# Linear attention and a routed feed-forward on one core: the routing stages run one slot nearer to the attention

## What is computed

```
x = x + attention(layernorm(x))      # 16 heads of 8, causal, scores without softmax: (Q K^T * causal) V, then w_o
x = x + experts(layernorm(x))        # logits = layernorm(x) @ Wg, softmax over 8 experts, the best 2 of each token
                                     # y = p * (relu(xs @ W1[e] + b1[e]) @ W2[e] + b2[e]), both choices added up
```

## Time and profile before

| | |
|---|---|
| median of 3 runs | 280.29 us (279.5 to 280.4) |
| the profiled execution | 280.46 us |
| its span, first to last instruction | 278.7 us |
| TensorE, busy share | 82% |
| VectorE | 73% |
| ScalarE | 61% |
| GpSimd | 65% |
| mean granted clock of TensorE | 0.916 |

### The profile page before, as it was taken

How to read it: one execution, slowest core, us unless ns; L and a number is a source line. 1 busy time by engine, 2 the same in 40 slices (tenths; PEclk the granted TensorE clock), 3 DMA queues, 4 the chain that set the end, 5 groups by cost and what they waited for, 6 DMA issues and landing times.

```text
span 278.7 us, 6426 instructions
## 1 busy us (share of the span) xinstructions
PE 227.6 (82%) x1418; PEld 175.7 (63%) x1418; DVE 202.1 (73%) x598; ACT 170.7 (61%) x675; POOL 182.0 (65%) x175
## 2 busy tenths in 40 slices
PE   6699889999999999998856279988919999999100
PEld 6354546666666666665545169877909999999000
DVE  5879999889989898999984848844502555554852
ACT  3543358888989898878697146655604767766000
POOL 3329961123868878687737777777777777777750
PEclk9999999999999999999995559999965999999855
DMA  6980000000100101011101272233445333438984
GB/s 203 280 246 0 2 1 0 2 0 12 41 30 30 41 30 42 29 38 39 51 29 48 67 166 69 59 105 103 115 131 142 107 98 88 125 101 294 330 228 136
DMA packets 32425, 25.49 MB, mean 91 GB/s; under 512 B 4334, under 2 KB 30192, under 8 KB 32390
## 3 DMA queue, kind: packets, MB, share of 16 engines
q1 hardware_dynamic: 23824, 14.52, 19.4%
q0 software_dynamic: 4320, 8.47, 9.1%
q10 hardware_dynamic: 4246, 2.10, 2.6%
HBM read 13.92 MB, written 11.61 MB: 92 GB/s over the span
## 4 chain that ended last, share of the span: by engine, by line
PE 55%; DVE 17%; DMA 10%; issue 8%; POOL 3%; ACT 3%; SPq 2%; POOLq 1%; DVEq 1%; ACTq 0%
PE ps L971 16%; PE ps L1063 8%; PE ps L1074 7%; PE ps L939 6%; DMA returned<-y_sb,xt 4%; POOL returned L417 3%; DVE back L680 3%; PE ps L980 2%; DMA xt<-dispatched 2%; PE ps L1056 2%; PE ps L991 2%; PE ps L962 2%; DVE back L671 2%; DVE o_sb L693 2%; PE ps L983 1%
## 5 line engine op out<-in xcount | busy, mean ns | idle before, releaser
L389 POOL DMA_INDIRECT dispatched<-rows,slot x64 | 65.8, 1028 | 37.5 <-ACT rows L482 17.0
L417 POOL DMA_INDIRECT returned<-y_sb,xt x71 | 71.1, 1002 | 21.6 <-issue 17.1
L971 PE MATMUL ps<-back,causal 128*128 128x512 f32 x128 | 61.9, 606 | 0.0
L881 DVE TENSOR_SCALAR y_sb<-ps,xt 128x128 f32<-128x128 f32 x71 | 24.9, 350 | 47.1 <-PE ps L1075 46.8
L1063 PE MATMUL ps<-xT,w_of 128*128 128x128 f32 x284 | 49.9, 301 | 1.2 <-DVE w_of L876 0.7
L1074 PE MATMUL ps<-w_sb,hT 128*128 x284 | 45.7, 285 | 0.1
L564 ACT ACTIVATE hT<-ps,b_col 128x128 f32<-128x128 f32 x142 | 44.2, 367 | 1.2 <-PE ps L1063 0.7
L373 POOL TENSOR_TENSOR back<-qkv 128x1024 f32<-128x1024 f32 x16 | 31.3, 1954 | 20.8 <-ACT qkv L503 20.6
L556 ACT ACTIVATE xT<-ps 128x128 f32<-128x128 f32 x71 | 19.7, 278 | 38.2 <-PE ps L1056 37.0
L1063 PEld LDWEIGHTS ps<-xT,w_of 128*128 128x128 f32 x284 | 39.8, 203 | 3.3 <-ACT xT L556 2.0
L680 DVE TENSOR_TENSOR back<-ps,qkv 128x1024 f32<-128x1024 f32 x32 | 38.9, 1216 | 2.1 <-PE ps L971 2.0
(11 more groups left out here) (171 smaller groups left out, 422.2 us busy)
## 6 DMA issues: line engine op xcount, KB each, us to landing
xt<-dispatched SPq DMA_DIRECT2D x71, 65.0 KB, 1.9
back<-returned SPq DMA_DIRECT2D x7, 512.0 KB, 6.4
x_sb<-x SPq DMA_DIRECT2D x8, 256.0 KB, 5.3
out<-x_sb ACTq DMA_DIRECT2D x7, 256.0 KB, 3.6
returned<-y_sb,xt POOLq DMA_INDIRECT x71, 2.5
w_sb<-w SPq DMA_DIRECT2D x1, 1024.0 KB, 5.7
w_sb<-w SPq DMA_DIRECT2D x2, 512.0 KB, 7.6
dispatched<-rows,slot POOLq DMA_INDIRECT x64, 2.3
```

The lines of the kernel that those rows point to most:

```text
L389: pool.indirect_dma_start(out=dispatched[:, :], out_offset=bass.IndirectOffsetOnAxis(ap=slot[:, g * K + k:g * K + k + 1], axis=0), in_=row ...
L417: pool.indirect_dma_start(out=returned[:, :], out_offset=bass.IndirectOffsetOnAxis(ap=xt[:, n % G, D:D + 1].bitcast(I32), axis=0), in_=y_s ...
L971: mm = pe.matmul(ps_run[g % 2][:, u, :], causal[:, :], outer[:, g % OUTER_RING, 512 * u:512 * (u + 1)], start=True, stop=True)
```

## The change

Every routing stage and every stage of the second normalization runs one slot earlier, on all engines: lags 10 to 13 of ScalarE become 9 to 12, 8 and 9 of VectorE become 7 and 8 (add_residual stays at 5), 10 to 12 of TensorE become 9 to 11, and dispatch(s - 16) becomes dispatch(s - 15). STATE_AFTER and the waits that name a tile go along. With that, softmax_end and places of batch 5 fall into VectorE's loop. In the tail VectorE makes the second statistics of the last six tiles, in two groups (26 and 27, then 28 to 31), and ScalarE's row_of is gone; softmax_start of batch 6 stands ahead of the last two tiles' residuals.

```
-    STATE_AFTER = 7
+    STATE_AFTER = 6
...
+    LAST = [range(N - 6, N - T), range(N - T, N)]
...
-            for s in range(N + 16):
-                if s >= 16:
-                    dispatch(s - 16)
+            for s in range(N + 15):
+                if s >= 15:
+                    dispatch(s - 15)
...
-            tile_stages = [(10, mean2_out), (12, exponentials), (10, spread2_out), (0, qkv_out), (10, variance_log2), (11, xn2T_out), (10, scale2_out),
-                           (-1, xnT_out), (10, shift2_out), (6, qT_out), (10, rows_out), (-2, normalize), (7, oT_out), (13, chosen),
+            tile_stages = [(9, mean2_out), (11, exponentials), (9, spread2_out), (0, qkv_out), (9, variance_log2), (10, xn2T_out), (9, scale2_out),
+                           (-1, xnT_out), (9, shift2_out), (6, qT_out), (9, rows_out), (-2, normalize), (7, oT_out), (12, chosen),
...
-            exponentials(N - 2 * T - 1)
-            xn2T_out(N - 8)
+            xn2T_out(N - 7)
             qT_out(N - 3)
+            chosen(N - 2 * T - 1)
             oT_out(N - 4)
             qT_out(N - 2)
-            row_of(N - 7)
             qT_out(N - 1)
             oT_out(N - 3)
-            chosen(N - 2 * T - 1)
-            row_of(N - 6)
+            last_deviation(0)
+            rows_out(N - 6)
             oT_out(N - 2)
-            row_of(N - 5)
+            rows_out(N - 5)
+            xn2T_out(N - 6)
             oT_out(N - 1)
-            xn2T_out(N - 7)
-            xn2T_out(N - 6)
             xn2T_out(N - 5)
-            last_deviation()
             exponentials(N - T - 1)
+            last_deviation(1)
...
-            tile_stages = [(5, add_residual), (9, softmax_end), (1, attend_sum), (8, softmax_start), (0, attend), (0, scales_ahead),
-                           (9, places), (2, state_out), (-2, outer_product), (-2, statistics_ahead)]
+            tile_stages = [(5, add_residual), (8, softmax_end), (1, attend_sum), (7, softmax_start), (0, attend), (0, scales_ahead),
+                           (8, places), (2, state_out), (-2, outer_product), (-2, statistics_ahead)]
...
             count_first()
+            add_residual(N - 5)
+            last_statistics(N - 6)
+            last_statistics(N - 5)
             state_out(N - 2)
-            add_residual(N - 5)
-            softmax_end(N - 2 * T - 1)
+            last_shift(0)
             attend_sum(N - 1)
             state_out(N - 1)
-            places(N - 2 * T - 1)
-            for g in range(N - T, N):
+            for g in range(N - 4, N - 2):
                 add_residual(g)
                 last_statistics(g)
-            last_shift()
             softmax_start(N - T - 1)
+            for g in range(N - 2, N):
+                add_residual(g)
+                last_statistics(g)
+            last_shift(1)
             softmax_end(N - T - 1)
...
-                wait(pe, shift_done, batches(g - 12))
+                wait(pe, shift_done, batches(g - 11))
...
-            tile_stages = [(3, running_sums), (11, gate), (5, q_transposed), (7, o_transposed), (5, sum_state), (-1, project),
-                           (-2, transpose1), (10, transpose2), (7, project_out), (12, rank)]
+            tile_stages = [(3, running_sums), (10, gate), (5, q_transposed), (7, o_transposed), (5, sum_state), (-1, project),
+                           (-2, transpose1), (9, transpose2), (7, project_out), (11, rank)]
```

More of the change, by code:

```diff
@@ L511, in exponentials, with last_deviation @@
                 act.activation(expd[:, :, :], shifted[:, :, :], ACT.Exp).then_inc(exp_done, 1)
[L513 to L517, removed]
+            def last_deviation(n):
+                own = LAST[n]
+                act.wait_ge(last_stats, own.stop - LAST[0].start)
+                act.activation(log2[:, own.start:own.stop], mv[:, own.start:own.stop, 1], ACT.Ln, bias=eps[:, 0:1]).then_inc(last_log, 1)
+                act.wait_ge(last_log, n + 1)
+                act.activation(norm2[:, own.start:own.stop, 0], log2[:, own.start:own.stop], ACT.Exp, scale=-0.5).then_inc(last_rstd, 1)
             def rows_out(g):
-                if g < N - T:
+                if g < LAST[0].start:
                     wait(act, norm2_done, g + 1)
                 else:
-                    act.wait_ge(last_norm, 1)
+                    act.wait_ge(last_norm, 1 + (g in LAST[1]))
                 wait(act, x2_done, g + 1)
@@ L701, in last_statistics, with last_shift @@
                 dve.bn_stats(stats[:, g, :], tile(g)).then_inc(last_raw, 1)
-                dve.wait_ge(last_raw, g + 1 - (N - T))
+                dve.wait_ge(last_raw, g + 1 - LAST[0].start)
                 dve.bn_aggr(mv[:, g, :], stats[:, g, :]).then_inc(last_stats, 1)
[L705 to L708, removed]
+            def last_shift(n):
+                own = LAST[n]
+                dve.wait_ge(last_rstd, n + 1)
+                dve.scalar_tensor_tensor(out=norm2[:, own.start:own.stop, 1], in0=mv[:, own.start:own.stop, 0], scalar=-1.0,
+                                         in1=norm2[:, own.start:own.stop, 0], op0=ALU.mult, op1=ALU.mult).then_inc(last_norm, 1)
             def softmax_start(g):
@@ L950, in q_transposed @@
                 wait(pe, qT_done, states(g) - 1)
-                wait(pe, xn2T_done, g - 5)
+                wait(pe, xn2T_done, g - 4)
                 pe.transpose(ps_qT, qkv[:, g % QKV_RING, 0:D], ident[:, :]).then_inc(qT_mm, 1)
@@ L978, in o_transposed @@
                 wait(pe, qT_done, states(min(g + 1, N - 1)))
-                wait(pe, xn2T_done, g - 3)
+                wait(pe, xn2T_done, g - 2)
                 mm = pe.matmul(ps_oT, o_sb[:, g % RING, :], ident[:, :], start=True, stop=(g % T == 0))
@@ L995, in transpose2 @@
                 wait(pe, rows_done, g + 1)
-                wait(pe, oT_done, g + 4, N)
+                wait(pe, oT_done, g + 3, N)
                 wait(pe, xn2T_done, g)
@@ L1001, in gate @@
                 wait(pe, xn2T_done, g + 1)
-                wait(pe, qkv_done, g + 12, N)
+                wait(pe, qkv_done, g + 11, N)
                 wait(pe, shift_done, batches(g - 1))
@@ L1015, in rank @@
                 wait(pe, before_done, b + 1)
-                wait(pe, x2_done, g + 5, N - T + 1)
+                wait(pe, x2_done, g + 4, N - T + 1)
                 wait(pe, placeof_done, b)
@@ L1099, in last_o_transposed @@
                 wait(pe, qT_done, states(N - 3))
-                wait(pe, xn2T_done, N - 7)
+                wait(pe, xn2T_done, N - 6)
                 mm = pe.matmul(ps_oT, o_sb[:, g % RING, :], ident[:, :], start=True, stop=(g % T == 0))
@@ L1144, in _ @@
             last_project_out(N - 3)
[L1145 to L1146 removed]
+            last_gate(N - 7)
+            last_transpose2(N - 6)
             last_o_transposed(N - 2)
[L1148 removed]
             last_project_out(N - 2)
[L1150 removed]
+            last_transpose2(N - 5)
+            last_gate(N - 6)
             last_o_transposed(N - 1)
+            last_gate(N - 5)
             last_project_out(N - 1)
[L1153 to L1156 removed]
             last_transpose2(N - 4)
```

17 lines of the change are left out of this document (1 added, 16 removed).

## The result

The changed kernel takes 300.18 us (median of 4 runs, 298.06 to 300.81), the kernel before 280.35 beside it: a ratio of 1.0705, interval 1.0632 to 1.0778. The profiled execution took 300.81 us.

The account below looks back on a forecast made before the run. GpSimd's chain from batch 5's dispatch was taken to bound the kernel. Four periods of 18.95 us (ring plus collision) delay that dispatch by 8.9, batch 6 adds 0.9: 280.46 + 8.9 + 0.9 = 290.3 us, range 281.5 to 292.5.

Parts of the forecast that it names:

- The bound: GpSimd's unbroken chain from batch 5's dispatch at 144.55 us to the end, started by VectorE's slots for that batch.
- The first pick: VectorE's first pick in the loop, forecast at 57.46 + 0.3 + 0.54 = 58.3 us.
- The ring: Pick waits for TensorE's sum_state, project for VectorE's `shifted`; period 17.35 instead of 15.98 us, project waiting 1.36 each.
- TensorE's side is 12.18: TensorE's own way from sum_state to project within a period after the change: 12.18 us, against VectorE's longer side.
- The collision: GpSimd's outer product starts 0.1 to 0.3 us before VectorE's second and holds it 1.6 us; period 18.95.
- The period becomes 13.54 + 3.81: Loop period as sum_state to project, 13.54 us, plus project to the next sum_state, 3.81: 17.35 instead of 15.98.
- Pick of batch 5: In VectorE's stretch from batch 4's pick to batch 5's slots, taken to run without a wait in 18.5 us.
- Batch 6: Its slots, late in VectorE's tail, miss GpSimd by an estimated 0.3 to 1.3 us; 0.9 taken.
- What lies behind: GpSimd's remaining work after the dispatches of batches 5 and 6, taken to move with them at unchanged length.
- Rival 2: The ring has room: project does not wait, period stays 15.98 us, dispatch 3.0 earlier, total 277.8; chance 0.10.

Follow-up runs that it names:

- e1: Changed kernel with GpSimd's outer product issued ahead of its dispatch in each slot; 287.95 us, ratio 1.030 to the kernel before.
- e4: Changed kernel with ten unused matmuls on TensorE ahead of project's wait for `shifted`, four times; 294.99 us, ratio 1.053.
- e9: Changed kernel with e6's tail, and batch 6's softmax_end and places ahead of residual, statistics and shift of tiles 30 and 31; 296.49 us, ratio 1.058.
- e11: e10 with the changed kernel's pick, which reads PSUM and waits for TensorE's sum_state; 279.42 us, ratio 0.9967.
- e10: Changed kernel with GpSimd's product before dispatch, pick from SBUF without wait, softmax_start second in VectorE's slot, e9's tail; 277.89 us, ratio 0.9889.
- e2: Changed kernel with pick always reading the experts' numbers from SBUF, never waiting for sum_state; 289.71 us, ratio 1.038.
- e6: Changed kernel, tail reordered: batch 5's places, count_first and statistics of tiles 26 and 27 before attend(31), their rows, transposes, gates before o_T; 302.78 us, 1.080.
- e7: Changed kernel with e1's edit and softmax_start as the first stage of VectorE's slot; 286.03 us, ratio 1.021.
- e12: Kernel before, with only GpSimd's outer product ahead of its dispatch and pick from SBUF without a wait; 280.62 us, ratio 0.9997.

## Why the prediction was right or wrong

- **The bound** (GpSimd's chain from batch 5's dispatch to the end): right. The dispatch moved by 17.18 us, batch 6's by 4.44 more, and all behind it took 1.27 less: 20.35 of 300.81 - 280.46.
- **The first pick**: forecast 58.3, found 57.79. Half a us of the surplus is missing there.
- **The ring**, 13.54 + 3.81 = 17.35: right, shown alone by e1 (13.47 + 3.88). Its other side was not: "TensorE's side is 12.18" was read in the old order, and is 12.9 in the new one. So project waits 0.60 us in e1 where 1.36 was forecast. This changes no period as long as VectorE's side is longer.
- **The collision**, "GpSimd is first by 0.1 to 0.3 and holds for 1.6": right that it comes four times, mis-sized. The holds were 2.08, 2.13, 1.75 and 1.75. VectorE's product ends 1.09 us after GpSimd's in all four, that is, it does its whole work behind it, wherever its own recorded start is. I had priced a hold from an assumed lead of GpSimd's start; in the first two periods VectorE's product is recorded 0.25 and 0.29 us ahead of GpSimd's, and was held longer. For that order the prediction had put the hold at nothing, so that it came in these two is luck. 4 times 0.33, 1.3 us.
- **The step that failed**: "The period becomes 13.54 + 3.81". The 3.81 from project to sum_state was read where TensorE never paused; behind a wait of 2.3 us or more it is 5.56. I had counted what is queued behind project as shifted, not as slower. The slow piece is TensorE at the lower of its two clocks. e4 gives 1.74 a period, four periods 7 us: the largest part of the miss. In a loop with the ring alone (e1) it does not come, as its wait is short.
- **Pick of batch 5** "without a wait": wrong, it waited 0.74 for sum_state (L959). The lower STATE_AFTER makes that batch read PSUM too, which is in the diff.
- **Batch 6**, "I estimate 0.3 to 1.3": measured 4.4. I reasoned from how nearly it had been late before, and did not write out VectorE's order in the tail. There gmax waits for the last gate, and the statistics of the last tiles, which wait for the attention's end, stand between the two halves of batch 6's softmax (2.5 and 2.2 us against e9). Before, that order cost nothing visible: batch 5's routing lay in the same stretch. 3.5 us.
- **What lies behind**, taken as unchanged, was 1.3 shorter.

Sum of the differences: -0.5 + 1.3 + 7 + 0.7 + 3.5 - 1.3 = 10.7, for the 10.5 between 290.3 and 300.81. A slip without weight: 24 dispatches have 23 steps from 144.55 to 175.52, so one takes 1.35 on average; the eight of batch 5 take 1.26 each.

**Rival 2** said that with VectorE's stretch under 12.18 the period would stay 15.98 and the time be 277.8. e11 comes close to the condition (pick to the end of `shifted` is 12.25 us, 11.8 without the wait for the gate, where 11.44 was needed) and has 16.8 and 279.4: VectorE waits for the gate there, and TensorE's side is 12.9. e10, where pick waits for nothing, took 277.9 with periods of 16.5: the same number, not by the sum that rival 2 made.

"SBUF — State Buffer", section "SBUF: two separate sides", of the Trainium skill (the lock for whole instructions) held here: all of VectorE's held instructions have two SBUF inputs (outer product, and pick from SBUF), and attend, with one in PSUM, was not: in e1 it took 1.21 us at 84.72, beside GpSimd's product of 83.77 to 85.73. That whoever comes first has the port can't be seen in the recorded starts: in two of the four periods VectorE's is the earlier one, and it was held all the same.

## What to carry to other kernels

When engines wait for each other in a ring, write out each side between its two waits before moving a stage: a slack of 0.2 us was all this loop had. Read each side in the new order, not in the old one. If the sum says that TensorE will stand still for 2.3 us or more, as it did here, price the time behind the wait at the lower clock too, from a row that shows it. In an epilogue written by hand, follow each in-order queue by name: an instruction that waits for other work, placed between two halves of the urgent chain, costs its wait.

## What the runs showed of the hardware

- **Wait and clock.** Waits of 2.29 to 2.74 us on TensorE, four of four, brought the clock down from 2.4 GHz towards 1.2 for a piece of each period (mean 0.92), and so did two of 2.83 and 2.66 in e2; those of 0.60 us in e1's loop never did. What lies between was not told apart.
- **The port.** The held instruction ends as if it had begun 0.1 us before the other's end (1.22 - 1.09), even with a recorded start 0.25 us ahead of GpSimd's (67.72 against 67.97). So the recorded start does not tell who has the port. The hold works the other way too: GpSimd's next dispatch took 1.81 us instead of 0.96, and ended 0.88 after VectorE's product did (112.98).
- **A start that differs.** In the 13 us before the attention's loop is full, a stretch that no edit touches, project waits twice for 0.5 to 1.1 us in all 14 traces. In nine of them, the two kernels' own among them, the granted clock stays at 1.00. In the other five (e6, e7, e10, e11, e12) it is 0.50 to 0.61 from 13.3 to 16.3 us: in e6's profiled execution the fourth project took 1.32 us at 13.34 instead of the changed kernel's 0.91 at 13.25, and the fifth starts 1.8 us later, at 17.77. Its first pick is 3.1 us later. The profiled executions of these five are 1.3 to 3.1 us above their kernels' medians. So part of the scatter of times comes from the start, and distances between picks compare better than their times.
